# Latent attention: the turn of sums and the last value product put in front of the split product of the same step

## The reference, cut to what matters

```python
H, QL, KVL, DN, DR, DV = 32, 192, 64, 128, 64, 128
c_q = x @ w_q_down; c_kv = x @ w_kv_down             # [1024, 192], [1024, 64]
q_lat  = einsum('bhsd,hdr->bhsr', q_nope, wuk)       # 64 latent dims per head
scores = (q_lat @ c_kv.T + rope(q_rope) @ rope(k_rope).T) / sqrt(192)
probs  = softmax(where(causal, scores, min))
out    = einsum('bhsr,hdr->bhsd', probs @ c_kv, wuv)
x      = layernorm(x + out.reshape(1, 1024, 4096) @ w_out)
```

## Time and profile before

| | before |
|---|---|
| three runs, median (lowest to highest) | 1512.86 us (1512.28 to 1513.26) |
| the profiled execution | 1512.49 us |
| its span | 1510.7 us |
| PE busy over the span | 1422.4 us (94%) |
| DVE busy | 939.8 us (62%) |
| ACT busy | 813.4 us (54%) |
| POOL busy | 533.9 us (35%) |
| first attention's 16 rounds | end at about 753 us |

### The profile page before, as it was taken

How to read it: one execution, slowest core, us unless ns; L and a number is a source line. 1 busy time by engine, 2 the same in 40 slices (tenths; PEclk the granted TensorE clock), 3 DMA queues, 4 the chain that set the end, 5 groups by cost and what they waited for, 6 DMA issues and landing times. The chain is left out here.

```text
span 1510.7 us, 23933 instructions
## 1 busy us (share of the span) xinstructions
PE 1422.4 (94%) x8048; PEld 1011.7 (67%) x8048; DVE 939.8 (62%) x1521; ACT 813.4 (54%) x1731; POOL 533.9 (35%) x495
## 2 busy tenths in 40 slices
PE   5699999999999999999977987999999999999997
PEld 4566776776677777677646874555555558888885
DVE  4455665555566555566668646766666427767967
ACT  3566766666666566666533322565565665333433
POOL 0134454333445443344042134404131024444442
PEclk9799999999999999999989998999999999999998
DMA  5233334333333433332410045534335032000000
GB/s 186 71 47 47 41 50 53 36 48 44 45 41 51 53 35 48 42 40 38 87 56 1 1 56 71 71 44 62 53 53 107 34 118 120 1 0 1 3 25 28
DMA packets 61666, 75.90 MB, mean 50 GB/s; under 512 B 20641, under 2 KB 42145, under 8 KB 60705
## 3 DMA queue, kind: packets, MB, share of 16 engines
q1 hardware_dynamic: 57248, 64.55, 24.6%
q0 software_dynamic: 4352, 10.49, 5.1%
HBM read 42.49 MB, written 2.10 MB: 30 GB/s over the span
## 5 line engine op out<-in xcount | busy, mean ns | idle before, releaser
L1682 DVE TENSOR_REDUCE pm<-l_sm 128x2 f32<-128x1024 f32 (+1 forms) x192 | 178.5, 956 | 96.0 <-PE l_sm L1556 59.9
L1642 ACT ACTIVATE l_probs<-l_banks 128x512 f32<-128x512 f32 (+3 forms) x366 | 165.6, 495 | 134.1 <-PE l_banks L1586 83.0
L666 ACT ACTIVATE probs<-sc,nmax 128x128 f32<-128x128 f32 (+7 forms) x256 | 190.1, 743 | 72.1 <-DVE nmax L750 68.1
L750 DVE TENSOR_REDUCE nmax<-sc 128x1 f32<-128x128 f32 (+7 forms) x256 | 193.5, 756 | 32.6 <-PE sc L493 27.1
L674 ACT COPY pt<-tb 128x512 f32<-128x512 f32 (+3 forms) x256 | 129.3, 505 | 151.1 <-PE tb L507 150.1
L507 PE MATMUL tb<-ident,probs 128*128 128x128 f32 x1152 | 172.5, 275 | 2.1 <-ACT pt L674 1.1
L78 PE MATMUL sc<-k_h,q_h 128*128 128x512 f32 (+4 forms) x384 | 144.4, 376 | 10.5 <-DVE q_l L774 8.7
L507 PEld LDWEIGHTS tb<-ident,probs 128*128 128x128 f32 x1152 | 132.1, 141 | 13.5 <-DVE pt L758 3.8
L1583 PE MATMUL l_banks<-qk_bufs 128*128 128x512 f32 (+3 forms) x366 | 134.8, 410 | 0.8 <-ACT l_probs L1642 0.4
L529 PE MATMUL mb<-pt,ckv 128*64 128x512 f32 (+2 forms) x736 | 131.7, 493 | 3.2 <-DVE x_tok L740 2.9
L78 PE MATMUL sc<-k_h,q_l 128*128 128x512 f32 (+4 forms) x384 | 132.4, 345 | 0.0
(11 more groups left out here) (288 smaller groups left out, 3107.7 us busy)
## 6 DMA issues: line engine op xcount, KB each, us to landing
gated_late<-in_gated SPq DMA_DIRECT2D x11, 768.0 KB, 13.2
wout<-in_w_out SPq DMA_DIRECT2D x16, 512.0 KB, 4.4
late<-late SPq DMA_DIRECT2D x128, 64.0 KB, 2.0
rb<-rT SPq DMA_DIRECT2D x248, 32.0 KB, 4.5
qk_bufs<-late SPq DMA_DIRECT2D x96, 64.0 KB, 5.7
qk_bufs<-late POOLq DMA_DIRECT2D x96, 64.0 KB, 6.7
nope_t<-in_nope_by_dim SPq DMA_DIRECT2D x16, 192.0 KB, 3.9
late<-in_gated SPq DMA_DIRECT2D x3, 768.0 KB, 7.9
```

Of the source, the lines that this page charges most:

```text
L666: act.activation(prob_row(n, s), score_row(n)[0], ACT.Exp, bias=nmax[:, s:s + 1], accum_out=ssum[:, n:n + 1]).then_inc(exped, 1)
L750: dve.tensor_reduce(nmax[:, n % 4:n % 4 + 1], row, axes, ALU.max, negate=True).then_inc(negmax, 1)
L1642: act.activation(probs[(NC * g + c) % RING][:, h, 0:w], e_slot(g, n)[:, 0:w], ACT.Exp).then_inc(exped, 1)
L1682: dve.tensor_reduce(pm[g % 2][:, :, s, i, half], slot(("m", g, n))[:, :, 0:w], AX.X, ALU.max, negate=True).then_inc(freed, 1)
```

## The change

The order of two items in three steps is swapped, for PE and for DVE: in step 1 `sums` 1 comes before `out` 1, in step 4 `values` 3 before `out` 3, in step 9 `sums` 0 before `query` 3 (on PE; DVE has only `sums` 0 there). Banks, waits, ACT's, POOL's and SP's lists stay as they are, and within a bank the order of the items is the same.

```diff
-        WORK = {0: [("out", 0)], 1: [("out", 1), ("sums", 1)], 2: [("values", 1), ("latent", 0)],
-                3: [("values", 2), ("out", 2)], 4: [("out", 3), ("values", 3)], 5: [("query", 0)], 6: [("query", 1)],
+        WORK = {0: [("out", 0)], 1: [("sums", 1), ("out", 1)], 2: [("values", 1), ("latent", 0)],
+                3: [("values", 2), ("out", 2)], 4: [("values", 3), ("out", 3)], 5: [("query", 0)], 6: [("query", 1)],
```

More of the change, by code:

```diff
@@ L282, in stage_mla @@
         QUERIES = [(1, 0), (1, 1), (0, 0), (0, 1)]
-        WORK = {0: [("out", 0)], 1: [("out", 1), ("sums", 1)], 2: [("values", 1), ("latent", 0)],
-                3: [("values", 2), ("out", 2)], 4: [("out", 3), ("values", 3)], 5: [("query", 0)], 6: [("query", 1)],
-                7: [("out", 4), ("out", 5)], 8: [("query", 2)], 9: [("query", 3), ("sums", 0)], 10: [("out", 6), ("out", 7)],
+        WORK = {0: [("out", 0)], 1: [("sums", 1), ("out", 1)], 2: [("values", 1), ("latent", 0)],
+                3: [("values", 2), ("out", 2)], 4: [("values", 3), ("out", 3)], 5: [("query", 0)], 6: [("query", 1)],
+                7: [("out", 4), ("out", 5)], 8: [("query", 2)], 9: [("sums", 0), ("query", 3)], 10: [("out", 6), ("out", 7)],
                 11: [("out_weights", 0)], 12: [("values", 0)]}
@@ L290, in stage_mla @@
                     13: [("split_out", 0)]}
-        DVE_WORK = {0: [("invert", 1), ("out", 0)], 1: [("out", 1), ("sums", 1)], 3: [("out", 2)],
-                    4: [("out", 3), ("values", 3)], 7: [("out", 4), ("out", 5)], 8: [("invert", 0)],
+        DVE_WORK = {0: [("invert", 1), ("out", 0)], 1: [("sums", 1), ("out", 1)], 3: [("out", 2)],
+                    4: [("values", 3), ("out", 3)], 7: [("out", 4), ("out", 5)], 8: [("invert", 0)],
                     9: [("sums", 0)], 10: [("out", 6), ("out", 7)], 11: [("out_weights", 0)], 12: [("values", 0)]}
```

## The result

| | before | after |
|---|---|---|
| median (lowest to highest), 4 runs each | 1512.57 us (1512.28 to 1513.26) | 1522.17 us (1519.13 to 1524.41) |
| ratio, 95% interval | | 1.0065 (1.0053 to 1.0077) |
| the profiled execution, span | 1512.49 us, 1510.7 us | 1519.13 us, 1517.3 us |

The account below looks back on a forecast made before the run. PE's stream was taken as the bound (busy 39.74 of 40 us). 14 x (0.49 + 0.13 + 0.02), plus 0.49 for round 0 and 0.13 for round 15, gave +9.6 us: 1522.4 us, range 1517.5 to 1526 (8 in 10).

Parts of the forecast that it names:

- Step 9: PE's `sums` 0 must wait for ACT's read of `query` 2 in bank 0: +0.49 us, 15 times.
- Step 1: `out` 1 ends one transpose later, so `values` 1 in its bank starts later: +0.13 us, 15 times.
- Step 4: The 0.28 us wait moves from `out` 3 to `query` 0 in step 5: net +0.02 us, 14 times.
- `rb`: Transfer DVE needs in step 4, forecast in time; rival (8 in 100): late, up to 0.4 us per full round.
- Regrouping at 0: Placing exact pieces beside other exact ones on PE priced at 0, between -0.1 and +0.1 us a round.
- Waits decide: Claim that waits on PE, not the regrouping of exact pieces, decide the change's effect, +9.6 us in sum.

Follow-up runs that it names:

- step9_only: The kernel before with only step 9 swapped (`sums` 0 ahead of `query` 3): 1519.80 us against 1512.04 before.
- half_on_dve: The changed kernel, but DVE reads the second half of `query` 2 in step 8, then ACT the first: 1518.13 us against 1512.04 before.
- half_beside: half_on_dve with both halves of `query` 2 read at once, PE waiting for both: 1516.02 us against 1512.00 before.
- invert_first: half_beside with the reciprocal of the sums put back ahead of DVE's half in step 8: 1513.81 us against 1511.51 before.
- steps1_4: The changed kernel with step 9 put back, so steps 1 and 4 swapped alone: 1512.46 us against 1512.04 before.
- no_waits: The kernel before with `sums` 1 ahead of `out` 1, `latent` 0 ahead of `values` 1, `out` 2 ahead of `values` 2: 1495.73 us against 1512.04.
- latent_grouped: no_waits with the four latent products sorted by width (128, 128, 64, 64 columns): 1493.18 us against 1512.00 before.
- weights_step12: latent_grouped with `out_weights` moved from step 11 to step 12, directly ahead of `values` 0: 1485.53 us against 1512.00 before.
- values_merged: weights_step12 with `values` 2 moved from step 3 to step 2, behind `values` 1: 1487.22 us against 1511.51 before.

## Why the prediction was right

- *Bound.* PE is the bound and its order decides: right. In all eleven kernels compared with the one before, 15 times the difference of the round gives the difference of the medians to within some 3 us.
- *Step 9.* The term of 0.49 measured 0.57, the only one off by more than 0.02. The wait itself was right (L515 at 0.94 us behind the turn, worked out 0.93); the restart was not: from L515 to the second row behind it are 0.41 us after a wait, 0.34 without. I had seen that a first row after a wait is longer in step 4 and did not carry it over to the transpose. step9_only shows the term alone, and half_on_dve, half_beside and invert_first show that it goes as the wait goes.
- *Step 1.* 0.13 forecast, 0.11 measured; steps1_4 agrees (0.10 in steps 1 and 2).
- *Step 4.* The gain of 0.28 that the covered wait offered is gone again in step 5, in front of `query` 0, as worked out: 0.02 forecast, 0.00 measured. In no_waits, where values stand between both pairs of output and query products on the same bank, steps 3 and 4 are 0.29 us shorter and the gain stays, as it must if the next user of the bank is what took it back.
- *`rb`.* In time, no term. The profile before had shown 15 waits of DVE for it in step 12, which the prediction did not mention; that PE does not wait for it was right.
- *Regrouping at 0.* Right for this change and shown twice, by step 1 (0.03 us from L515 to the next start in either place) and by invert_first. The number type of the turn's neighbours does not matter. But my argument looked at the wrong property, and "Waits decide" was too wide: a border that costs exists on PE, between products of 64 and of 128 columns. The change leaves the number of these borders as it was, two in step 4 in either order, so the zero held, and in part by luck. Step 4 compares two orders with the same borders and says nothing of their price. It stood in the rows all the same: behind one transpose the first value product starts after 0.20 us, a float32 product of 128 columns after 0.11 (398.43 to 398.54 in no_waits). I had charged the transpose 0.03 and called the rest, 0.17, an entry. The page of the Trainium skill named in the prediction ("TensorEngine Tiling (Array Packing)", section "Key Properties") says that a change of tiling mode drains TensorE; I used it to say that nothing is won here, and it pointed to the larger gain: latent_grouped, with such changes removed and nothing else, is 0.29 us a round faster, which agrees with it. Not every change of width costs, though: the turn of sums has 8 columns (128*8) between products of 128 and takes what one more transpose takes, 0.11 us. Which property sets the price, the width, the place in the array or the weight load, no run separates, and what the hardware does inside was not measured.
- *Sum.* 14 x 0.64 + 0.62 = 9.6 forecast, 14 x 0.65 and about 0.6 = 9.7 by the rounds, 9.6 by the medians. The terms and the mechanism were right; that the totals agree to a tenth is luck, since the interval is 3.6 us wide and the 0.08 too little in step 9 stands against 0.02 too much in each of steps 1 and 4.

Still open: why the executions of one kernel spread (before 1507.3 to 1514.6 us over the runs beside the experiments). The profiled ones differ in the start and in what lies behind the score of step 11 in round 15, mostly the unchanged layers: 773.0 us after and 774.3 us before; what makes them differ there was not looked into.

## What to carry to other kernels

When two pieces of a step are exchanged, look up for each who used its buffer last and how long that reader still needs, and who uses it next: a wait that is covered in one place is often only handed on to the next user of the same bank. Order the pieces of a bounding engine by these waits, not by likeness of type. When they are grouped, group them by what the engine pays for, which is read from start to start of the same instruction behind different neighbours.

## What the runs showed of the hardware

- A border between PE products of 64 and of 128 output columns costs: behind one transpose a 64-wide product starts after 0.20 us and a 128-wide one after 0.11; a pair of L456 records takes 0.37 us behind a 64-wide product and 0.26 behind a 128-wide one; two borders taken away are worth 0.29 us a round in latent_grouped, 0.33 in weights_step12 and 0.24 in values_merged. The transpose of 8 columns between products of 128 shows no such price (invert_first: 0.44 us behind four transposes' start, 0.03 us to the next product).
- A border between float32 transposes and fp32r matmuls costs nothing (0.11 us for one more transpose in either surroundings).
- After a wait of half a microsecond PE's first instruction takes 0.05 us more until the next one starts (0.08 against 0.03 for L515), and the second row behind it is 0.07 us late in all. The granted clock stayed at 1.00 through these waits (after, 440 to 480 us).
- A wait can stand in the profile as "issue" with no releaser: in half_beside the weight load of L518 started 0.22 us behind the end of the reciprocal, with two register instructions of PE in between. With a wait on the product's own instruction it is 0.05 to 0.06 us (L515 after, `query` 0 after).
